# Experts' first layer with the weights as the stationary operand, loaded per tile

## The reference, cut to what matters

```
gate_up = x @ gate_up_w[e].T        # x: 128 features; gate_up_w[e]: 352 x 128
h       = silu(gate_up[:176]) * gate_up[176:]      # 176 wide
y       = h @ down_w[e].T           # down_w[e]: 128 x 176
out[token] = sum over the two chosen experts of weight * y
```

## Time and profile before

| what | value |
|---|---|
| three runs | 871.68, 871.88, 870.04 us (median 871.68) |
| span of the profiled execution (the page gives no other time for it) | 869.2 us |
| TensorE busy, share, records | 806.7 us, 93%, 4810 |
| VectorE | 647.6 us, 74% |
| ScalarE | 518.5 us, 60% |
| GpSimd | 526.1 us, 61% |
| moved by DMA | 61.81 MB, 71 GB/s |
| DMAs issued by SyncE (the page's list of issues, added up) | some 200 |

### The profile page before, as it was taken

The page is one execution under the profiler, slowest core; times in us unless marked ns, Lnnn a source line. Parts: engine busy times, 40 slices in busy tenths (PEclk is TensorE's granted clock), DMA queues, the critical chain, the costliest instruction groups (busy, mean ns, idle before and its releaser), DMA issues.

```text
span 869.2 us, 16114 instructions
## 1 busy us (share of the span) xinstructions
PE 806.7 (93%) x4810; PEld 613.1 (71%) x4810; DVE 647.6 (74%) x2260; ACT 518.5 (60%) x1057; POOL 526.1 (61%) x610
## 2 busy tenths in 40 slices
PE   7999999999999999999989998899899899999893
PEld 6668586757768578677777676686677675785772
DVE  5397688898586866778767958899999588576435
ACT  3887757667777876766756544467473356354241
POOL 3159474668544475683666254876637775757753
PEclk9999999999999999999999999999999999999997
DMA  9920000000101111120122112212212241241333
GB/s 302 397 111 2 1 2 1 2 11 31 34 13 38 43 46 32 49 71 26 40 77 76 53 58 79 71 45 87 63 41 73 71 143 44 81 142 56 97 117 121
DMA packets 62069, 61.81 MB, mean 71 GB/s; under 512 B 7835, under 2 KB 53531, under 8 KB 61771
## 3 DMA queue, kind: packets, MB, share of 16 engines
q1 hardware_dynamic: 52387, 40.94, 15.4%
q0 software_dynamic: 9312, 19.17, 6.9%
q10 hardware_dynamic: 288, 0.67, 0.3%
HBM read 27.46 MB, written 33.30 MB: 70 GB/s over the span
## 4 chain that ended last, share of the span: by engine, by line
PE 35%; DVE 22%; POOL 16%; issue 13%; DMA 6%; ACT 6%; SPq 1%; DVEq 0%; POOLq 0%; ACTq 0%
PE psum L564 6%; PE psum L833 6%; POOL sent_y L1836 5%; PE psum L853 4%; POOL sorted_l L1795 3%; DVE xs L1333 2%; POOL sorted_x L1795 2%; PE psum L644 2%; PE psum L783 2%; PE psum L768 2%; PE psum L773 2%; DVE l_place L1308 2%; DMA sorted_l<-m_cv,r_slot 1%; ACT f_xn L1437 1%; PE psum L688 1%
## 5 line engine op out<-in xcount | busy, mean ns | idle before, releaser
L1836 POOL DMA_INDIRECT sent_y<-e_y,l_to x115 | 111.9, 973 | 62.4 <-DVE e_y L1293 33.3
L833 PE MATMUL psum<-gu_w,e_sx 128*128 x368 | 125.2, 464 | 2.6 <-DVE e_y L1293 1.2
L1795 POOL DMA_INDIRECT sorted_l<-m_cv,r_slot x80 | 77.5, 969 | 44.5 <-issue 21.0
L853 PEld LDWEIGHTS psum<-d_w,e_h 88*128 88x128 f32 x736 | 91.4, 191 | 17.8 <-issue 13.9
L853 PE MATMUL psum<-d_w,e_h 88*128 x736 | 99.2, 278 | 3.6 <-ACT e_h L1442 1.2
L1442 ACT ACTIVATE e_h<-psum 88x512 f32<-88x512 f32 x96 | 54.2, 572 | 63.6 <-PE psum L564 61.6
L1622 ACT ACTIVATE e_h<-psum 128x352 f32<-128x352 f32 x96 | 42.6, 450 | 79.4 <-PE psum L833 79.1
L833 PEld LDWEIGHTS psum<-gu_w,e_sx 128*128 128x128 f32 x368 | 63.8, 190 | 31.9 <-issue 11.2
L1289 DVE TENSOR_TENSOR e_h<-e_h,psum 128x352 f32<-128x352 f32 x96 | 47.6, 501 | 32.7 <-ACT e_h L1622 32.1
L1823 POOL DMA_INDIRECT c_y<-sorted_y,r_slot x48 | 48.4, 1009 | 29.1 <-DMA sorted_y<-e_y 11.9
L1722 POOL TENSOR_TENSOR m_seg<-w_scan,m_dt 128x512 f32<-128x512 f32 x32 | 36.3, 1135 | 47.0 <-PE psum L712 38.7
(11 more groups left out here) (246 smaller groups left out, 2088.5 us busy)
## 6 DMA issues: line engine op xcount, KB each, us to landing
m_cv<-sorted_l SPq DMA_DIRECT2D x55, 130.0 KB, 2.2
sorted_l<-c_y SPq DMA_DIRECT2D x10, 512.0 KB, 14.8
c_y<-sent_y SPq DMA_DIRECT2D x20, 256.0 KB, 4.0
e_sx<-sorted_x SPq DMA_DIRECT2D x33, 128.0 KB, 2.2
sorted_y<-e_y SPq DMA_DIRECT2D x33, 128.0 KB, 1.9
sorted_l<-c_y SPq DMA_DIRECT2D x5, 471.0 KB, 14.5
xs<-in_x SPq DMA_DIRECT2D x8, 256.0 KB, 7.0
sorted_x<-c_y SPq DMA_DIRECT2D x4, 512.0 KB, 14.4
```

The source lines that it names most:

```text
L833: last = e.matmul(two.banks[j].tile[:, 0:2 * IEXP], e_xT[k % 4][:, j * P:(j + 1) * P], gu_w[:, bass.ds(which[j] * (2 * IEXP), 2 * IEXP)], ...
L853: last = e.matmul(bank.tile[:, j * P:(j + 1) * P], e_hT[s][0:IHALF, (2 * j + c) * P:(2 * j + c + 1) * P], d_w[:, bass.ds(which[j] * (2 * D ...
L1795: e.indirect_dma_start(out=sorted_l[SENT_GROUPS.index(g)] if g in SENT_GROUPS else sorted_x[n], out_offset=bass.IndirectOffsetOnAxis(ap=r_ ...
L1836: e.indirect_dma_start(out=sent_y[n], out_offset=bass.IndirectOffsetOnAxis(ap=l_to[n][:, 2 * t + j:2 * t + j + 1], axis=0), in_=e_y[k % 4] ...
```

## The change

The first layer is made turned. Now the expert's weights are the stationary operand and the turned rows are streamed, so the product comes out with hidden units on partitions and tokens along the free axis, which is what the second layer needs. A tile takes three matmuls of 128 columns: 128 gate units, the rest (48 up units on partitions 0 to 47 and 48 gate units on partitions 64 to 111, with zeros between), and 128 up units. The first two go to one PSUM bank (signal `e_ga`), the third to another (`e_gu`). The turning of the product, its bank and ScalarE's copy are gone. The silu and the multiply are two instructions each, one for the 128 units and one for the 48. The second layer takes 128 rows and then 112 of the product, instead of twice 88; the padding rows of `e_h` are set to zero once by GpSimd.

`gu_w` is no longer in SBUF. A new SyncE piece `weights(g, t)` reads each tile's expert from `r_expert` into a register and loads its 128 x 368 weights (188 KB) from DRAM into one of four buffers, on the same semaphore as the rows. The ranks of most stages are new, and the rank of the result copy (L1293) goes from T + 12.0 to T + 10.5.

```diff
-FIRST = [-6.0, 20.1, 58.2, 69.3, 100.4, 125.5, 150.6, 175.7]
+FIRST = [-12.0, 41.1, 57.2, 73.7, 100.7, 124.9, 150.6, 175.7]
...
-SORTED_AT = [7.0, 7.0, 7.0, 4.0, -1.0, -1.0, -1.0, 24.0]
-PAIR_AT = [23.9, 23.9, 23.9, 26.9, 65.9, 17.9, 77.9, 65.9]
+SORTED_AT = [2.0, 7.3, 5.4, 4.3, -2.7, -61.7, 3.0, -48.3]
+PAIR_AT = [23.9, 23.6, 26.6, 28.9, 65.9, 61.9, 71.9, 82.9]
-COMBINED_AT = [19.3, 25.3, 0.3, 19.3, 4.3, 2.3, 7.3, 4.3]
-KV_AT = [104.8, 147.8, 197.8, 141.8, 147.8, 135.8, 147.8, 150.8]
-SECOND_AT = [176.0, 209.0, 208.0, 281.0, 431.0, 426.0, 545.0, 515.0]
-GATED_AGAIN_AT = [37.0, 37.0, 37.0, 37.0, 47.0, 47.0, 47.0, 47.0]
+COMBINED_AT = [21.6, -4.7, 0.3, 19.3, 39.3, 4.3, -49.0, 34.3]
+KV_AT = [62.8, 141.5, 187.5, 131.1, 155.8, 174.1, 146.5, 150.8]
+SECOND_AT = [207.7, 208.0, 207.0, 277.0, 431.0, 402.0, 532.7, 462.0]
+GATED_AGAIN_AT = [29.3, 70.0, 70.0, 43.7, 97.0, 76.0, 7.0, 22.0]
...
-SEND_AT = [150.0, 125.0, 252.0, 159.0, 158.0]
+SEND_AT = [147.1, 116.0, 266.7, 254.7, 314.7]
...
 # TensorE, experts(g, t)
                 for j in range(m):
-                    last = e.matmul(two.banks[j].tile[:, 0:2 * IEXP], e_xT[k % 4][:, j * P:(j + 1) * P],
-                                    gu_w[:, bass.ds(which[j] * (2 * IEXP), 2 * IEXP)], start=True, stop=True)
+                    e.matmul(bank.tile[:, j * P:(j + 1) * P], gw[:, j, 0:P], xT[:, j * P:(j + 1) * P], start=True, stop=True)
+                    last = e.matmul(bank.tile[0:EW - REST_AT, (2 + j) * P:(3 + j) * P], gw[:, j, REST_AT:EW],
+                                    xT[:, j * P:(j + 1) * P], start=True, stop=True)
+                last.then_inc(*S.up("e_ga"))
+                bank.freed = ("e_h", k + 1)
+                yield T + 5.6, 0.46, ("bank", 1), ("e_ga", k + 1)
+                bank = banks.take(("e_gu", k))
+                on.wait_ge(*bank.freed)
+                for j in range(m):
+                    last = e.matmul(bank.tile[:, j * P:(j + 1) * P], gw[:, j, UP_AT:UP_AT + P], xT[:, j * P:(j + 1) * P],
+                                    start=True, stop=True)
                 last.then_inc(*S.up("e_gu"))
...
-                transposes(bank, lambda c: e_h[s][:, c * IHALF:(c + 1) * IHALF], 2 * m, IHALF).then_inc(*S.up("e_trh"))
-                bank.freed = ("e_hT", k + 1)
...
 # VectorE, experts(g, t)
-                e.tensor_tensor(h, h, banks.tile("e_gu", k)[:, 0:m, IEXP:2 * IEXP], ALU.mult).then_inc(*S.up("e_h"))
-                yield T + 12.0, 0.42, ("e_down", k + 1), stored(k)
+                on.wait_ge("e_silu", 2 * k + 1)
+                on.wait_ge("e_gu", k + 1)
+                e.tensor_tensor(most, most, banks.tile("e_gu", k)[:, 0:m * P], ALU.mult)
+                on.wait_ge("e_silu", 2 * k + 2)
+                e.tensor_tensor(rest, rest, banks.tile("e_ga", k)[0:IREST, 2 * P:(2 + m) * P], ALU.mult).then_inc(*S.up("e_h"))
+                yield T + 10.5, 0.42, ("e_down", k + 1), stored(k)
...
 # ScalarE, experts(g, t)
-                e.activation(h, banks.tile("e_gu", k)[:, 0:m, 0:IEXP], ACT.Silu).then_inc(*S.up("e_silu"))
-                yield T + 9.7, 0.6, ("e_trh", k + 1)
-                on.wait_ge("e_trh", k + 1)
-                copy(e_hT[s][0:IHALF, 0:2 * m * P], banks.tile("e_hT", k)[0:IHALF, 0:2 * m * P], "e_hT")
+                e.activation(e_h[s][:, 0:m * P], bank[:, 0:m * P], ACT.Silu).then_inc(*S.up("e_silu"))
+                e.activation(e_h[s][0:IREST, 2 * P:(2 + m) * P], bank[GATE_AT:GATE_AT + IREST, 2 * P:(2 + m) * P],
+                             ACT.Silu).then_inc(*S.up("e_silu"))
...
 # SyncE
+            def weights(g, t):
+                k = g * PAIRS + t
+                yield PAIR[g][t] - 2.0, 0.5, ("r_expert", g + 1), ("e_gu", k - 3)
+                on.wait_ge("r_expert", g + 1)
+                on.wait_ge("e_gu", k - 3)
+                for j in range(pair_tiles(t)):
+                    expert = e.value_load(r_expert[g % 2][0:1, 2 * t + j:2 * t + j + 1], min_val=0, max_val=E1 - 1)
+                    e.dma_start(e_gw[k % 4][:, j, :], d["gu_w"][:, bass.ds(expert * EW, EW)]).then_inc(*S.up(f"sx{k % 4}", 16))
+                yield None
```

More of the change, by code:

```diff
@@ L427, in build @@
         e_xT = turned(e_sx)
+        e_gw = ring("e_gw", [P, 2, EW], 4)
         e_h = ring("e_h", [P, 2 * 2 * P])
-        e_hT = e_h
         e_y = ring("e_y", [P, 2, DM], 4)
@@ L478, in m_ln_parts, with expert_loads, loads_before @@
             return t[:, 24:32].rearrange("p (j s) -> p j s", s=2), two(32), two(40), two(48), t[:, 56:60]
-        def expert_loads(e):
-            return 16 * (e // 4 + 1)
+        def expert_loads(k):
+            return 16 * sum(1 + pair_tiles(x % PAIRS) for x in range(k % 4, k + 1, 4))
+        def loads_before(slot, k):
+            return 16 * sum(1 + pair_tiles(x % PAIRS) for x in range(slot, k, 4))
         def given(i):
@@ L750, in gates @@
                 bank.freed = ("g_xT", i + 1)
-                yield (T + 5.5, 0.8, ("bank", 1), ("w_late", 16 * 4), ("g_xT", i + 1), ("s_res", i - 1),
+                yield (T + 5.5, 0.8, ("bank", 1), ("w_late", 16 * 3), ("g_xT", i + 1), ("s_res", i - 1),
                        ("c_add", GB * (i // GB - 1)), ("r_rank", i // GB - 1))
@@ L755, in gates @@
                 keep_busy(bank)
-                on.wait_ge("w_late", 16 * 4)
+                on.wait_ge("w_late", 16 * 3)
                 on.wait_ge("g_xT", i + 1)
@@ L837, in experts @@
                     numbers(g, t + 1)
-                two.frees("e_h", k + 1)
-                yield T + 9.0, 0.43, ("bank", 1), ("e_h", k + 1)
-                bank = banks.take(("e_hT", k))
+                bank.freed = ("e_h", k + 1)
+                yield T + 9.0, 0.93, ("bank", 1), ("e_h", k + 1), stored(k)
+                bank = banks.take(("e_y", k))
                 on.wait_ge(*bank.freed)
@@ L843, in experts @@
                 on.wait_ge("e_h", k + 1)
-                transposes(bank, lambda c: e_h[s][:, c * IHALF:(c + 1) * IHALF], 2 * m, IHALF).then_inc(*S.up("e_trh"))
-                bank.freed = ("e_hT", k + 1)
[L846 to L850, removed]
+                which = expert_of.pop(k)
                 for j in range(m):
-                    for c in range(2):
-                        last = e.matmul(bank.tile[:, j * P:(j + 1) * P], e_hT[s][0:IHALF, (2 * j + c) * P:(2 * j + c + 1) * P],
-                                        d_w[:, bass.ds(which[j] * (2 * DM) + c * DM, DM)], start=(c == 0), stop=(c == 1))
+                    y = bank.tile[:, j * P:(j + 1) * P]
+                    e.matmul(y, e_h[s][:, j * P:(j + 1) * P], d_w[:, bass.ds(which[j] * (2 * DM), DM)], start=True, stop=False)
+                    last = e.matmul(y, e_h[s][0:EW - REST_AT, (2 + j) * P:(3 + j) * P],
+                                    d_w[0:EW - REST_AT, bass.ds(which[j] * (2 * DM) + DM, DM)], start=False, stop=True)
                 last.then_inc(*S.up("e_down"))
@@ L868, in attn_kv @@
                 for j in T4:
-                    yield T + 5.5 + 0.7 * j, 0.64, ("bank", 1), ("k_qkv", 4 * b + j), ("k_ctx", b - 1), ("w_late", 16 * 4), ("k_xT", b + 1)
+                    yield T + 5.5 + 0.7 * j, 0.64, ("bank", 1), ("k_qkv", 4 * b + j), ("k_ctx", b - 1), ("w_late", 16 * 3), ("k_xT", b + 1)
                     bank = banks.take(("k_qkv", 4 * b + j))
@@ L1861, in gpsimd_program @@
             e.memset(ones_b[:, :], 1.0)
+            for n in range(2):
+                e.memset(e_h[n][:, 2 * P:4 * P], 0.0)
             for n in range(2):
@@ L1916, in sync_program @@
                 load_block(b)
-            for name, tile, kilobytes in (("gu_w", gu_w, 1408), ("d_w", d_w, 704)):
-                issued(kilobytes)
-                e.dma_start(tile[:, :], d[name]).then_inc(*S.up("w_late", 16))
+            load("d_w", d_w[:, :], 1024, "w_late")
             load("w_attn", w_attn[:, :], 520, "w_late")
@@ L1994, in store @@
                 yield None
-            return ([experts(g, t) for g in range(ROUNDS * NGROUP) for t in range(PAIRS)]
+            return ([weights(g, t) for g in range(ROUNDS * NGROUP) for t in range(PAIRS)]
+                  + [experts(g, t) for g in range(ROUNDS * NGROUP) for t in range(PAIRS)]
                   + [sent_rows(i, t0, m) for i in SENT_BLOCKS
```

77 lines of the change are left out of this document (40 added, 37 removed).

## The result

The changed kernel takes 960.5 us (median of 4 runs, 959.9 to 964.5); the kernel before has 871.8 beside it (4 runs). The ratio is 1.103, 95% interval 1.100 to 1.106: 89 us slower, where 19 us faster were forecast and 879 was the end of the range. The span of its profiled execution is 958.8 us.

The account below looks back on a forecast made before the run. TensorE was taken as the bound from 250 to 456 us, nearly full with VectorE from 560 to 789, GpSimd's chain after. Span 869.2 - 15.2 (TensorE) - 4.0 (ranks) = 850.0; with 2.5 us for run time, 852.5 us; range 828 to 879.

Parts of the forecast that it names:

- the one on SyncE: SyncE and DMA queues: added weight loads fit in SyncE's free time and bandwidth, cost 0, bounds 0 to +9 us.
- slower: the SyncE queue: Rival: weight loads waiting in SyncE's single order hold up rows, stores and reads; 882 to 892 us, chance 0.16.
- TensorE, per tile: First layer on TensorE: three 128-column matmuls take 0.675 us a tile instead of 0.81, 24.8 us less over 184 tiles.
- What of it lies on the path: Share of TensorE's saving that shortens the run, counted by stretches: 15.2 us, bounds -5.5 and 24.8.
- VectorE and ScalarE: Second multiply adds 0.32 us a pair on VectorE, partly hidden; ScalarE's copied and silu columns fall from 864 to 512, hidden.
- Ranks: New order on every engine: -4 us, for one hole in GpSimd's tail; bounds -18 and +27 us.
- four signs of being wrong: Loads releasing tens of us of TensorE waits; longer tail; fillers above 60 us with little time gained; short matmuls at 0.3 us or more.
- The signs of being right: Matmuls 0.225 us apart, silu under 0.45, VectorE above 90% somewhere late, hardly any idle from loads, tail 76 us or less.

Follow-up runs that it names:

- c5: Changed kernel with its order held on the other engines, without per-tile weight loads (fixed tiles loaded once at the start): 900.0 us, 1.029.
- c4: Changed kernel planned with load costs near those measured (1.75 us for a pair's weights, 0.5 for a row load, 3.3 to landing): 913.7 us, 1.047.
- e12: Kernel before, with the planner told 0.52 us instead of 0.50 for the pair's multiply, giving another order on every engine: 992.4 us, 1.026.
- e13: c4 with the first layer's matmuls of a pair in one stage asking for two banks at once: 980.1 us, 1.012.
- e6: Changed kernel without any weight loads during the run (fixed tiles), planned anew without them: 904.0 us, 1.035.
- e11: e3 again, the kernel before with the changed kernel's ranks: 994.7 us, 1.027.
- e5: Same kernel as c4, the changed kernel planned with nearly true load costs, in a group where the kernel before takes 967 us: 1002.0 us, 1.031.
- e9: e6 with VectorE's second multiply of every pair (48 x 256) left out, order of all else held: 903.9 us, 1.034.
- e3: Kernel before with the changed kernel's ranks and nothing else: 994.3 us, 1.025.
- e7: e6 with the ranks of the kernel before: 939.2 us, 1.076.
- c1: The changed kernel again as a control, in a group where the kernel before takes 967 us: 1028.5 us, 1.061.
- e4: Changed kernel with all ranks of the kernel before and one more wait on VectorE: 1087.6 us, 1.116.
- e2: Changed kernel keeping SyncE's waits, reads and issues, each weight load cut to 16 of 128 partitions: 1021.0 us, 1.053.

## Why the prediction was wrong

**The step that failed** is the one on SyncE: "The weights are asked for 2 us of rank ahead and three pairs deep, 7.5 us at the tail's pace of two sends a pair, so I take 0. The upper bound is +9 us". The loads cost some 60 us with the order held: 960.5 less c5's 900.0. Three things in the step were wrong. The price of a pair was 1.3 us and is 2.15, with 0.43 for the rows behind it: to a read of 0.27 us and an issue of 0.33 come 0.24 us of address arithmetic and moves, and 0.25 of gaps between the instructions, per tile. More important, I asked whether SyncE has time to spare (it has) where the question was what stands between a freed buffer and the landing of the rows: "three pairs deep" says how many buffers there are, not how early a load starts, since each load starts only when the pair three back has ended, and in the place shown TensorE stood still for 4.8 us in two gaps. And I took what TensorE waits for today as a bound of what a new chain can make it wait for; nothing supports such a bound. The rival *slower: the SyncE queue* had the mechanism and a chance of 0.16, but put 5 us on a group and left out both the pairs within a group and the clock.

**What made it so dear was probably in the diff, and I did not price it:** the planner was told 0.5 us for the weights of a pair and 0.0 for the row load, against 2.15 and 0.43. Told 1.75 and 0.5, and a later landing, it makes a plan in which the same loads on the same engine stand at 1.047 instead of 1.103, 49 of the 89 us less. That this is due to the costs being nearer the truth is likely, as TensorE's waits for the rows go with it, and not shown: c4 is another order throughout, and e12 and e13 move by 2.6 and 1.9% through changes of the plan alone. For the same reason what the loads would cost in a plan that knows them is known only roughly: 1.8% over c5 and 1.2% over e6, both in other orders. Without loads 25 us remain (c5's 1.029). That they are the loss of the order that the old ranks fitted is likely and not shown: e11 and e12 lose 2.7 and 2.6% in the kernel before by ranks or plan alone, which is as much, but in the group where that kernel takes 968 us. e13 is lower than e5 with the first layer in one stage; whether that is the split or another lucky order can't be told. How the 25 us divide stays open.

**TensorE, per tile: right.** The short matmuls start 0.22 us apart, as taken (timeline of an ordinary pair; a group of x2 is one matmul):

```profile
501.91 0.39 PE L838 MATMUL psum<-e_sx,e_gw 128*128 128x128 f32 x2
502.13 0.38 PE L839 MATMUL psum<-e_sx,e_gw 128*112 128x128 f32 x2
502.35 0.39 PE L838 MATMUL psum<-e_sx,e_gw 128*128 128x128 f32 x2
502.57 0.38 PE L839 MATMUL psum<-e_sx,e_gw 128*112 128x128 f32 x2
502.79 0.96 PE L765 MATMUL psum<-w_gates,g_xT 128*128 128x9 f32 x8
```

Work at full clock fell by 17.5 us (19.3 in c5), seven tenths of the 24.8 forecast, to 727 where 725 was named; where the other 7 us went is not known. The Trainium skill ("TensorE: Matmul & The Clock Gate", section "Back-to-back issue gap") would have made short matmuls dearer per column; these f32 rows say no: 0.22 us at 128 columns where the earlier trace rows have 0.59 at 352.

**What of it lies on the path: wrong.** 15.2 us were counted because TensorE was full. The change itself ended that, and no run shows that the gain bought anything: even without any load (e6, c5) the turned form is slower.

**VectorE and ScalarE: right in duration**, and VectorE's second multiply also in being hidden (e9; for ScalarE no run tests it). 48 partitions cost what 128 do at the same 256 columns (mean ns behind the busy time):

```profile
L1299 DVE TENSOR_TENSOR e_h<-e_h,psum 128x256 f32<-128x256 f32 x88 | 36.5, 415 | 28.0 <-PE psum L847 24.5 <-ACT e_h L1634 2.0 <-ACT e_h L1635 0.6
L1301 DVE TENSOR_TENSOR e_h<-e_h,psum 48x256 f32<-48x256 f32 x88 | 35.7, 405 | 0.0
L1634 ACT ACTIVATE e_h<-psum 128x256 f32<-128x256 f32 x88 | 33.7, 383 | 119.8 <-PE psum L839 119.0
L1635 ACT ACTIVATE e_h<-psum 48x256 f32<-48x256 f32 x88 | 33.5, 381 | 2.2
```

**Ranks: wrong in kind.** I priced them as an edit of their own, -4 us. A list of ranks has a worth only with its plan: the new ones cost the kernel before 2.5 to 2.7% (e3, e11) and are worth 4% to the turned form without loads (e6 against e7) and 5% to the changed kernel (c1's 1.061 against e4's 1.116, in two groups).

**The clock was in no term.** 39 of the 89 us are TensorE at 1.2 GHz. A warning stands in the same page of the Trainium skill, section "HAM oscillation — how this bites in real kernels": a kernel whose TensorE keeps waiting for DMA falls back to the lower clock again and again. The trace agrees: 4 stretches and 21.0 us at the half level before, 24 and 106.7 after; and in the table above the kernels that idle 91 to 95 us pay 23 to 29 for the low clock, those with 62 and 127 us 5 and 45.

Of the four signs of being wrong three came: loads as releasers of tens of us, a longer tail, fillers above 60 (60.9). The fourth, short matmuls at 0.3 us, did not. The signs of being right came where they stood for one engine's work (0.22 us a matmul, 0.38 a silu, VectorE 93% busy from 640 to 680 us), and failed where they stood for waiting and for the tail.

## What to carry to other kernels

Price a new wait by the chain from what releases it to what is late, in the order in which one queue issues it, and not by the queue's free time; the waits of today are no bound for it. Where a planner fixes the order, look at the cost that it is told for each new piece before anything else, and expect a few per cent from any change of plan alone: take such a loss off with a run of the old kernel in a nudged plan before blaming the edit. And when TensorE is full at the full clock, a microsecond of idle can cost more than one, for the clock falls behind it: here 64 us more of idle time came with 39 more for the low clock.

## What the runs showed of the hardware

A load whose address comes from a register takes SyncE 1.09 us a tile here from one to the next, and only 0.33 of it is the issue. Bytes hardly counted: with an eighth of them the ratio is 1.053 for 1.061 (e2 and c1, in two groups, the intervals overlapping). A multiply or a silu of 48 partitions takes what one of 128 does (405 for 415 ns, 381 for 383). In the groups where the kernel before took 967 to 971 us, single places of 5 to 18 us appeared in which ScalarE or VectorE stood still, put down in the trace to no signal or to one from outside it, with TensorE idle beside them, while GpSimd went on (in e3 ScalarE for 17.7 us before 720.6 and TensorE for 15.0). What they are is not known. The record has the same chip number for the first group (971 us) and the third (872), so it need not be the chip.
